# Even and odd columns in the first stage of an attention and feed-forward kernel, fewer transfers, and another order of the attention's first loads

## What is computed

```python
xn = (x - mean) / sqrt(var + 1e-5)                       # x: (4, 2048, 256)
q, k, v = xn @ Wq + bq, xn @ Wk + bk, xn @ Wv + bv       # 16 heads of 16
q, k = rope(q), rope(k)          # rot: (x0, x1) -> (-x1, x0) for each pair of columns; x*cos + rot*sin
att = softmax(q @ k.T / sqrt(256)) @ v @ Wo + bo
h = relu(s0 * concat(xn, -xn) @ sign(k0)) * 2            # to 1024
h = relu(s1 * h @ sign(k1)) * 2                          # to 1024
out = x + att + s2 * h @ sign(k2)
```

## Time and profile before

| | |
|---|---|
| median of 3 runs | 2738.48 us (2738.41 to 2739.38) |
| the profiled execution, its span | 2738.91 us, 2737.1 us |
| PE, ACT, DVE, POOL busy | 97%, 76%, 36%, 11% of the span |
| chain that ended last | PE 86% of the span |
| granted TensorE clock, mean | 0.988 |

### The profile page before, as it was taken

One profiled execution on the slowest core, in us unless ns is written; L12 is line 12 of the kernel. 1 busy time (PEld: TensorE's weight loads), 2 busy tenths in 40 slices (PEclk: granted clock), 3 DMA queues, 4 the chain that ended last, 5 costly groups with the idle time before them and its releaser, 6 DMA issues.

```text
span 2737.1 us, 49717 instructions
## 1 busy us (share of the span) xinstructions
PE 2648.9 (97%) x21063; PEld 1397.6 (51%) x21063; DVE 989.5 (36%) x1655; ACT 2083.9 (76%) x2301; POOL 299.0 (11%) x265
## 2 busy tenths in 40 slices
PE   7999499999999999999999999999999999999997
PEld 5777245454444445454545454454545454544544
DVE  7776232324242323232342334242423323242322
ACT  4556388888888887878787878888787878787883
POOL 4666100000000000000000000000000000000000
PEclk9999699999999999999999999999999999999998
DMA  8888412212222222222221222221222222222213
GB/s 256 256 259 252 114 38 55 53 52 59 59 59 59 73 54 72 55 60 72 57 71 55 72 67 75 57 77 51 73 63 55 68 60 67 63 75 59 81 26 112
DMA packets 288416, 228.67 MB, mean 84 GB/s; under 512 B 184128, under 2 KB 227904, under 8 KB 281664
## 3 DMA queue, kind: packets, MB, share of 16 engines
q1 hardware_dynamic: 279744, 217.08, 29.0%
q10 hardware_dynamic: 8448, 8.39, 0.9%
...
## 4 chain that ended last, share of the span: by engine, by line
PE 86%; issue 1%; SPq 1%; DMA 1%; DVE 0%; POOLq 0%; POOL 0%; DVEq 0%
PE ps_o L930 35%; PE ps_f L963 26%; PE ps_s L915 23%; PE ps_y L978 2%; PE ps_f L1020 0%; SPq L810 0%; DMA xT_lo<-xn_lo_d 0%; DMA probs<-rest_sum_d 0%; PE ps_y L1020 0%; DVE k_rows L1115 0%; PE ps_o L1020 0%; SPq L807 0%; DVE sums L1060 0%; DMA heads_t<-heads 0%; SPq L709 0%
## 5 line engine op out<-in xcount | busy, mean ns | idle before, releaser
L895 ACT ACTIVATE probs<-ps_s 128x1024 f32<-128x1024 f32 x2048 | 1930.0, 1033 | 472.4 <-PE ps_s L915 470.1
L930 PE MATMUL ps_o<-probs,v_ones 128*32 128x512 f32 x8192 | 1011.9, 600 | 0.0
L915 PE MATMUL ps_s<-q_rows,k_rows 50*128 50x512 f32 x4096 | 866.3, 439 | 31.8 <-DMA q_rows<-row_shift 31.0
L915 PEld LDWEIGHTS ps_s<-q_rows,k_rows 50*128 50x128 f32 x4096 | 365.0, 184 | 701.9 <-ACT probs L895 600.0
L1077 DVE COPY raw<-ps_f 128x512 f32<-128x512 f32 x256 | 165.0, 686 | 790.8 <-PE ps_f L963 790.8
L930 PEld LDWEIGHTS ps_o<-probs,v_ones 128*32 128x32 f32 x8192 | 200.7, 109 | 418.5 <-issue 296.0
L963 PE MATMUL ps_f<-h_hi,ffn_w 64*128 64x512 f32 x2048 | 406.9, 393 | 0.0
L963 PE MATMUL ps_f<-h_lo,ffn_w 64*128 64x512 f32 x2048 | 405.8, 391 | 0.0
L1039 POOL TENSOR_TENSOR heads<-heads,sums 128x512 f32<-128x512 f32 x64 | 82.4, 1288 | 2147.9 <-DVE sums L1060 2147.9
L1060 DVE RECIPROCAL sums<-sums 128x128 f32<-128x128 f32 x256 | 226.7, 924 | 1.7
L963 PEld LDWEIGHTS ps_f<-h_lo,ffn_w 64*128 64x128 f32 x2048 | 195.8, 186 | 37.3
...
## 6 DMA issues: line engine op xcount, KB each, us to landing
k_rows<-k_parts SPq DMA_DIRECT2D x128, 256.0 KB
...
q_parts<-parts SPq DMA_DIRECT2D x32, 512.0 KB, 3.7
k_parts<-parts SPq DMA_DIRECT2D x32, 512.0 KB, 5.5
k_rows<-k_parts SPq DMA_DIRECT2D x128, 128.0 KB
x_chunk<-in_x ACTq DMA_DIRECT2D x16, 512.0 KB, 6.0
xn_hi_d<-xn_hi SPq DMA_DIRECT2D x16, 512.0 KB, 4.4
xn_lo_d<-xn_lo SPq DMA_DIRECT2D x16, 512.0 KB, 5.2
```

The lines of the kernel that those rows point to most:

```text
L895: nc.scalar.activation(probs[:, s % PBUF, half * 2 * C:(half + 1) * 2 * C], ps_s[:, half].rearrange("p c n -> p (c n)"), ACT.Exp, scale=SC ...
L915: last = nc.tensor.matmul(ps_s[:, half, w], k_rows[rows, u, t * P:(t + 1) * P], q_rows[rows, u, half], start=True, stop=True)
L930: last = nc.tensor.matmul(ps_o[32 * c:32 * c + 2 * DH], v_ones[:, u, t], probs[:, s % PBUF, c * C:(c + 1) * C], start=(t == 0), stop=(t == ...
```

## The change

q and k: `project` now makes the even columns and the odd columns of all heads once each, 24 matmuls a chunk, and the rotation combines them (`products` takes each of the two blocks for both outputs; POOL subtracts for one and adds for the other). The arrays in DRAM hold 4 x 8 rows a head in place of 2 x 16, and the chunks of q are stored in another order (`COLUMNS`), so that a half of a query row is one run. The normalised x is stored once, as full fp32 (ACT copies it, `copy_x`), in one run of 4 KB a partition, and split again on DVE in `attend` (`split_x`, in round 24 of the pass before; the first by itself). v is stored in one run of 4 KB a partition and loaded with 4 transfers a head. `bn_aggr` takes the place of five small operations. v has its own PSUM banks and is made in two halves. The order of each engine in a chunk is new, with `sums` and `normalise` one chunk further ahead, and the feed-forward weights are made over chunks 4 to 11. POOL sets `k_rows` to one at the start of `prepare`. `attend` first loads rows, v and x, then the constants, and the second head only after the first rows and x have landed. `shift` is stored by 4 transfers of 128 rows in place of one of 64.

```diff
+FFN_WEIGHTS_AT = 4
+FILL = 256
+FILLS = 16 * (G * N // (P * FILL))
+COLUMNS = [CB // 2 * (r % 2) + r // 2 for r in range(CB)]
+HALF = DH // 2
+SPLIT_AT = 2 * len(BURSTS) + 4
...
@@ prepare: SP
+    def store_shift(a):
+        to = scratch["shift"][a].rearrange("g (h w n) -> w (g h) n", h=P // G, n=FILL)
+        for n in range(G * N // (P * FILL)):
+            sp.dma_start(to[n], fill[:].bitcast(F32)).then_inc(fill_stored, 16)
...
     def store_x(c):
         u = c % 2
-        sp.wait_ge(x_split, c + 1)
-        sp.dma_start(hi_out[c], x_hi[:, u].bitcast(F32)).then_inc(x_stored[u], 16)
-        sp.dma_start(lo_out[c], x_lo[:, u].bitcast(F32)).then_inc(x_stored[u], 16)
+        sp.wait_ge(x_copied, c + 1)
+        sp.dma_start(scratch["xn"][c], x_t[:, u].rearrange("p k n -> p (k n)")).then_inc(x_stored[u], 16)
...
+        to = q_out[b, j, COLUMNS[r]] if j < 2 else k_out[b, j % 2, r]
+        sp.dma_start(to, parts[:, u].bitcast(F32)).then_inc(parts_stored[u], 16)
     store_x(0)
     for c in range(NC):
         if c > 0:
+            store_parts(4 * c - 2)
             store_parts(4 * c - 1)
-        sp.wait_ge(v_ready, c + 1)
-        sp.dma_start(v_out[c // CB, c % CB], v_sb[:, c % 2].rearrange("p h t d -> p h (t d)")).then_inc(v_stored[c % 2], 16)
+        if c + 1 < NC:
+            store_x(c + 1)
         store_parts(4 * c)
         store_parts(4 * c + 1)
-        if c + 1 < NC:
-            store_x(c + 1)
-        store_parts(4 * c + 2)
+        sp.wait_ge(v_ready, 2 * c + 2)
+        sp.dma_start(scratch["v"][c], v_sb[:, c % 2].rearrange("p h t d -> p (h t d)")).then_inc(v_stored[c % 2], 16)
...
@@ prepare: ACT
+    def copy_x(c):
+        u = c % 2
+        if c >= 2:
+            act.wait_ge(x_stored[u], 16 * (c // 2))
+        nc.scalar.activation(x_t[:, u].rearrange("p k n -> p (k n)"), ps_t[:].rearrange("p k n -> p (k n)"),
+                             ACT.Copy).then_inc(x_copied, 1)
...
+        act.wait_ge(v_done, 2 * c + half + 1)
+        if c >= 2 and half == 0:
             act.wait_ge(v_stored[u], 16 * (c // 2))
-        nc.scalar.activation(v_sb[:, u].rearrange("p h t d -> p t h d"), ps_v.rearrange("p t (h d) -> p t h d", d=DH),
+        t = slice(half * TT // 2, (half + 1) * TT // 2)
+        nc.scalar.activation(v_sb[:, u, :, t].rearrange("p h t d -> p t h d"), ps_v[:].rearrange("p t (h d) -> p t h d", d=DH),
...
+    copy_x(0)
     deviation(1)
+    normalise(1)
+    deviation(2)
     act.wait_ge(weights_loaded, 16 * 6)
     for c in range(NC):
         if c > 0:
+            part(4 * c - 2)
             part(4 * c - 1)
-        values(c)
-        if c + 1 < NC:
-            normalise(c + 1)
-        part(4 * c)
-        part(4 * c + 1)
         if c + 1 < NC:
             high(c + 1)
+            copy_x(c + 1)
+        values(c, 0)
+        part(4 * c)
         if c + 2 < NC:
-            deviation(c + 2)
-        part(4 * c + 2)
-        if c == NC - CB:
-            act.wait_ge(d0_ready, 1)
-            act.wait_ge(signs_ready, 1)
-            act.wait_ge(ffn_loaded, 16 * 6)
-        if c >= NC - CB:
-            ffn_weights(c % CB)
+            normalise(c + 2)
+        part(4 * c + 1)
+        if c + 3 < NC:
+            deviation(c + 3)
+        if FFN_WEIGHTS_AT <= c < FFN_WEIGHTS_AT + FT:
+            ffn_weights(c - FFN_WEIGHTS_AT)
+        values(c, 1)
...
@@ prepare: PE
         if c > 0:
-            pe.wait_ge(v_ready, c)
+            pe.wait_ge(x_split, c)
+            pe.wait_ge(x_copied, c)
...
-        c, j = n // 4, n % 4
+        c, of = n // 2, n % 2
...
         if n >= 2:
-            pe.wait_ge(products_ready, n - 1)
-        for swapped in range(2):
+            pe.wait_ge(products_ready, 2 * n - 2)
+        for m in range(2):
             for k in range(DT):
-                at = slice((j % DT) * P, (j % DT + 1) * P)
-                w_hi, w_lo = wqk_hi[:, swapped, j // DT, k, at], wqk_lo[:, swapped, j // DT, k, at]
-                to = ps_p[:, n % 2, swapped]
+                w_hi, w_lo = wqk_hi[:, of, k, m], wqk_lo[:, of, k, m]
+                to = ps_p[:, n % 2, m]
...
     for c in range(NC):
-        project(4 * c)
-        values(c)
+        project(2 * c)
+        if c + 1 < NC:
+            turn(c + 1)
+        values(c, 0)
+        project(2 * c + 1)
+        values(c, 1)
         if c > 0:
             lengths(c - 1)
-        project(4 * c + 1)
-        project(4 * c + 2)
-        if c + 1 < NC:
-            turn(c + 1)
-        project(4 * c + 3)
...
@@ prepare: POOL
+    nc.gpsimd.memset(w["k_rows"][:].bitcast(F32), 1.0)
...
+    for m in range(2):
+        for n in range(2):
+            nc.gpsimd.tensor_tensor(wqk_lo[:, n, :, m], of_pairs[:, n, :, :, m], wqk_hi[:, n, :, m].bitcast(F32), ALU.subtract)
...
-        nc.gpsimd.tensor_tensor(turned[:, n % 3], by_cos[:, u], by_sin[:, u], ALU.add).then_inc(turn_done, 1)
+        nc.gpsimd.tensor_tensor(turned[:, n % 3], by_cos[:, u], by_sin[:, u], ALU.add if n % 2 else ALU.subtract).then_inc(turn_done, 1)
...
@@ prepare: DVE
-        nc.vector.tensor_tensor(mean2[:, u], even, odd, ALU.add)
-        nc.vector.tensor_tensor(diff[:, u], even, odd, ALU.subtract)
-        nc.vector.tensor_tensor(var[:, u], stats[:, u, :, 2], stats[:, u, :, 5], ALU.add).then_inc(stat_step, 1)
-        dve.wait_ge(stat_step, 2 * c + 1)
-        nc.vector.scalar_tensor_tensor(out=diff[:, u], in0=diff[:, u], scalar=D / 4.0, in1=diff[:, u],
-                                       op0=ALU.mult, op1=ALU.mult).then_inc(stat_step, 1)
-        dve.wait_ge(stat_step, 2 * c + 2)
-        nc.vector.tensor_tensor(var[:, u], var[:, u], diff[:, u], ALU.add).then_inc(var_ready, 1)
+        for t in range(TT):
+            last = nc.vector.bn_aggr(moments[:, u, t], stats[:, u, t])
+        last.then_inc(var_ready, 1)
...
-        c, j, u = n // 4, n % 4, n % 2
-        dve.wait_ge(proj_ready, n + 1)
+        c, pair, out, u = n // 4, n // 2, n % 2, n % 2
+        if out == 0:
+            dve.wait_ge(proj_ready, pair + 1)
         if n >= 2:
             dve.wait_ge(turn_done, n - 1)
-        nc.vector.scalar_tensor_tensor(out=by_cos[:, u], in0=ps_p[:, u, 0], scalar=bqk[:, 0, j:j + 1], in1=cos[:, here(c)],
+        of = pair % 2
+        nc.vector.scalar_tensor_tensor(out=by_cos[:, u], in0=ps_p[:, of, out], scalar=bqk[:, of, out:out + 1], in1=cos[:, here(c)],
                                        op0=ALU.add, op1=ALU.mult)
-        nc.vector.scalar_tensor_tensor(out=by_sin[:, u], in0=ps_p[:, u, 1], scalar=bqk[:, 1, j:j + 1], in1=sin[:, here(c)],
+        nc.vector.scalar_tensor_tensor(out=by_sin[:, u], in0=ps_p[:, of, 1 - out], scalar=bqk[:, of, 1 - out:2 - out], in1=sin[:, here(c)],
                                        op0=ALU.add, op1=ALU.mult).then_inc(products_ready, 1)
...
-        dve.wait_ge(x_high, c + 1)
+        dve.wait_ge(x_copied, c + 1)
...
     for c in range(NC):
         products(4 * c)
+        products(4 * c + 1)
+        if c + 1 < NC:
+            low(c + 1)
+        if c + 3 < NC:
+            sums(c + 3)
+        products(4 * c + 2)
+        if c + 3 < NC:
+            factors(c + 3)
+        products(4 * c + 3)
         if c > 0:
             keep_norms(c - 1)
-        products(4 * c + 1)
-        if c + 2 < NC:
-            sums(c + 2)
-        products(4 * c + 2)
-        if c + 1 < NC:
-            low(c + 1)
-        products(4 * c + 3)
-        if c + 2 < NC:
-            factors(c + 2)
...
@@ load_rows and attend
-    return (scratch[name].rearrange("a (g d) n -> g a d n", d=DH) for name in ("k", "q"))
+    return (scratch[name].rearrange("am (g e) n -> g am e n", e=HALF) for name in ("k", "q"))
...
-    shift = scratch["shift"].rearrange("a g (h w n) -> g w a h n", w=2, n=C)
-    q_half = scratch["q"].rearrange("a (g d) (h w n) -> g a w d h n", d=DH, w=2, n=C)
+    shift = scratch["shift"].rearrange("a g (w n) -> g w a n", w=2)
+    q_flat = q_rows.rearrange("p h n -> p (h n)")
     for w in range(2):
 at = GROUP_ROWS * w
+here = slice(w * N // 2, (w + 1) * N // 2)
 sp.dma_start(k_rows[at:at + 2 * DH, :].bitcast(F32), k_head[g]).then_inc(loaded, 16)
-sp.dma_start(k_rows[at + 2 * DH:at + AUG, :].bitcast(F32), k_head[g, 0]).then_inc(loaded, 16)
-sp.dma_start(q_rows[at:at + DH].bitcast(F32), q_half[g, 0, w]).then_inc(loaded, 16)
-sp.dma_start(q_rows[at + DH:at + 2 * DH].bitcast(F32), q_half[g, 0, w]).then_inc(loaded, 16)
-sp.dma_start(q_rows[at + 2 * DH:at + AUG].bitcast(F32), q_half[g, 1, w]).then_inc(loaded, 16)
-sp.dma_start(q_rows[at + AUG:at + ROWS].bitcast(F32), shift[g, w]).then_inc(loaded, 16)
+sp.dma_start(k_rows[at + 2 * DH:at + AUG, :].bitcast(F32), k_head[g, 0:2]).then_inc(loaded, 16)
+sp.dma_start(q_flat[at:at + DH].bitcast(F32), q_head[g, 0:2, :, here]).then_inc(loaded, 16)
+sp.dma_start(q_flat[at + DH:at + 2 * DH].bitcast(F32), q_head[g, 0:2, :, here]).then_inc(loaded, 16)
+sp.dma_start(q_flat[at + 2 * DH:at + AUG].bitcast(F32), q_head[g, 2:4, :, here]).then_inc(loaded, 16)
```

(39 more changed lines are left out.)

143 lines of the change are left out of this document (67 added, 76 removed).

## The result

The changed kernel takes **2670.81 us** (median of 4 runs, 2669.19 to 2672.23); the kernel before takes 2738.93 us (4 runs, 2738.41 to 2740.60) beside it. The ratio is 0.975, 95% interval 0.9733 to 0.9767: 2.5% faster. The profiled execution of the changed kernel took 2669.19 us, its span is 2667.4 us, against a span of 2737.1 us before: 69.7 us less.

The account below looks back on a forecast made before the run. PE was taken to bound both stages, with a chain through ACT, DVE and POOL deciding `prepare` after the change. Terms -71.7 - 3.3 + 0.3 - 1.5 + 7.5 = -68.7 us against 2738.9 gave 2670 us, range 2648 to 2712 us.

Parts of the forecast that it names:

- The chain of a chunk (11.7 us): `prepare`: the chain through ACT, DVE and POOL, closed by POOL's addition, sets a chunk's period, 11.7 us against 16.38.
- The signs' block: `prepare`: the block of the signs takes 4.6 us of DVE once, now in a full chain: 3 us.
- The transfers shrink from 4.0 to 3.5 MB a chunk, all in long runs but the load of x; at the 403 GB/s of a slice full of 2 KB runs that is 9.1 us: `prepare`: a chunk's transfers need 9.1 us, near the other resources' 10 us, so the chain decides.
- rival 3: `prepare`: a longer chain, as by held `bn_aggr` or late stores, at 14 us: +28 us, 2698 us; chance 10%.
- The term of `prepare`: To the end of the last `turned`: -75.0 us predicted, with 15 periods giving -71.7 and the start -3.3.
- The start and the end of `prepare`: Half the lower parts of the weights at the start: -3.3 us; the block's end, shorter `fill`, three more SP issues: +0.3 us.
- The start of `attend`: Memset's 3.47 us go, but outer counts limit engines, rows take 19.0 us instead of 12.7: -1.5 us, between -7 and +5.
- Each pass of `attend` (+7.5 us): `attend`: late x holds DVE's split and PE stalls 0.5 us a pass, 15 passes: +7.5 us, between 0 and 47.
- the delay of x: `attend`: x, issued behind SP's held store and slower rows, comes 3.7 us later, between 2.3 and 6.3.
- my slack of 3.15 us: `attend`: x may come 3.15 us later for nothing before DVE's copy delays PE's next group.
- Rival 1: `attend`: x so late that `prepare`'s gain is lost, from 5.1 us of stall a pass; 2768 us at 7 us; 4%.
- Rival 5: `prepare`: PE, now with gaps, is granted 1.2 GHz: +121 us, 2791 us, slower; chance 1%.

Follow-up runs that it names:

- runs 1: Changed kernel, but of v and the turned x only chunk 0 is stored, and `attend` reads that chunk everywhere: 2658.53 us (ratio 0.9707).
- run 7: Changed kernel with key rows' setting back in `attend`, three buffers for loaded x, eight for parts, `d0` in the split weights' tile: 2666.06 us (0.9731).
- run 3: Changed kernel with DVE's `low` starting after `high`, and ACT's plain copy of x moved behind the first half of v: 2683.08 us (0.9796).
- run 4: Changed kernel with the setting of the key rows to one put back on DVE at the start of `attend`: 2673.92 us (0.976).
- run 9: Changed kernel with every transfer of key and query rows cut into pieces of 8 rows: 2661.19 us (0.9721).
- run 10: Changed kernel with each pass's x issued only after PE's ten steps of the third head, about 5.8 us later: 2768.24 us (1.0106).

## Why the prediction was right in the sum, and where its steps failed

**The chain of a chunk (11.7 us)** was right, in its path and to 0.3 us: 11.39 us from chunk 8 on where no transfer interferes (runs 1 and 7). These rows of run 7 show the stretch between the third and the fourth product in two periods, which begin with `high` at 142.56 and at 153.95:

```profile
148.84 1.30 POOL L503 TENSOR_TENSOR turned<-by_cos,by_sin 128x512 f32<-128x512 f32 x1 [1.06 <-DVE by_sin L550]
149.78 0.18 DVE L535 RECIPROCAL rstd<-std 128x4 f32<-128x4 f32 x1 [1.02 <-ACT std L319]
149.99 0.16 DVE L537 SCALAR_TENSOR_TENSOR shift_ln<-moments,rstd 128x4 f32<-128x4 f32 x1
...
160.22 1.30 POOL L503 TENSOR_TENSOR turned<-by_cos,by_sin 128x512 f32<-128x512 f32 x1 [1.06 <-DVE by_sin L550]
160.60 0.18 DVE L535 RECIPROCAL rstd<-std 128x4 f32<-128x4 f32 x1 [0.46 <-ACT std L319]
160.82 0.72 DVE L537 SCALAR_TENSOR_TENSOR shift_ln<-moments,rstd 128x4 f32<-128x4 f32 x1
```

In both, POOL's addition follows the third product, and `shift_ln` ends with it, at 150.15 and 161.54, as the prediction had it; the fourth product, POOL and the fourth part close the period. POOL waits for DVE as foreseen, 1.06 us ahead of the third sum and 0.18 us ahead of the fourth. What the prediction lacked is the branch through ACT that run 3 laid open. It arrives at nearly the same time: in the first period DVE waits 1.02 us for the square root and `shift_ln` then needs only its own 0.16 us, in the second the root is there 0.6 us earlier, and the period is the same. That this branch costs no more than 0.1 us here is luck. In the sum itself, 7.75 + 0.17 + 1.30 is 9.2 and not the 9.0 of the text; `bn_aggr` x4 takes 0.38 us with POOL at work beside it, where I had 0.45.

Smaller terms of the stage were off. The signs' block makes two periods of 13.95 and 13.18 us in run 7, 4.3 us more than two of 11.4, where I had 3 us. Of the three periods of 10.2 us at the end only the last came (10.17); the two before it are 11.39 and 11.38 us. And in two of the eight chunks that make feed-forward weights ACT works 2.7 us on them (79.50 to 82.16 in run 7), where I had 1.4 us and let them fit into its wait: these periods are 12.23 and 12.30 us.

**"The transfers shrink from 4.0 to 3.5 MB a chunk, all in long runs but the load of x; at the 403 GB/s of a slice full of 2 KB runs that is 9.1 us"** is the step that failed in `prepare`. The bytes did not turn out to be the bound, but the slice is the best of many, and I took from it that transfers in a shorter period would be as quick as before. The landings went from 3.8 to 7.0 us and from 6.1 to 9.4 us. With two buffers for x and four for the parts that is too late in five of the eleven periods: 12.30 us on average from chunk 4 to 15 in place of the 11.44 of run 7 ((186.89 - 61.02) / 11, chunk 4 at 61.02), 11 x 0.86 = 9.5 us. It is the "stores that come back late" of my rival 3, and the load of x beside them, with a smaller price than its 28 us, and I gave it 10% beside a forecast that should have contained it. The term of `prepare` was 9.6 us too good for that.

**The start and the end of `prepare`** were about right: the first projection comes at 14.98 us in place of 18.42, 3.4 us earlier (predicted 3.3). From the last `turned` to SP's load I had 3.2 us less, measured are 4.8; run 4 shows 4.3 of it as the key rows' setting.

**The start of `attend`** stood on the outer count. The rows took 20.7 us from SP's first load to the first scores, where I had 1.5 + 19.0 us, and the feed-forward network began 28.1 us behind that load, where I had 28.3. Run 9 shows the outer count at work: with 8 rows outside, the share of 232 to 236 us goes from 0.20 to 0.50 and 7.6 us come back. The rule of the Trainium skill (DMA: Bandwidth & Descriptors, section "Why a DMA increments its semaphore by 16 and not by 1") gives 8 of 16 engines for it, and the trace agrees. One detail was off: DVE's split waited for `bo`, the last transfer of all (it landed at 254.1), not for x (252.4).

**Each pass of `attend` (+7.5 us)** was wrong: the passes are 1.3 us shorter in all. The mechanism is there, as run 10 shows, but it never starts. In the seventh pass, shifted by 70.25 us (PE's next group, 1307.84 in the earlier trace rows, is at 1237.59):

```profile
1225.82 3.94 SPq L833 DMA_DIRECT2D heads_t<-heads  x4
1229.87 0.35 SPq L827 DMA_DIRECT2D xT_lo<-xn_d  x1
```

```profile
1233.47 0.69 DVE L1084 CAST xT_hi<-xT_lo 128x1024 fp32r<-128x1024 f32 x1 [15.79 <-DMA xT_lo<-xn_d]
...
1235.34 1.28 DVE L1103 COPY raw<-ps_f 128x512 f32<-128x512 f32 x2
```

x is issued 1229.87 + 70.25 - 1297.38 = 2.7 us later than before, not 3.7; it lands in 3.6 us, not 4.1; and PE goes on when the first bank is copied, as run 10 shows, 0.6 us earlier than I counted. So DVE idles 15.79 us and its copy starts 1.6 us before it would cost anything. The step that failed is the delay of x, 3.7 us against 2.7 measured: this alone is less than my slack of 3.15 us and leaves no stall. The slack was too small as well; it is 3.8 us.

**The rivals.** Rival 1 is real but was priced too low. I had it decide from 5.1 us of stall a pass; with the clock's share it is 5.1 x 4.0 / 6.5 = 3.1 us. Rival 5 did not come: PE stayed near full clock in `prepare`, 0.99 between 35 and 195 us, though some of its gaps were longer than the 2 us that I named (3.70 us before 49.31, 3.29 us before 83.21). The forecast held because 10 us of late transfers were set off by 9 us of stalls that did not happen. That is luck, and the range, not the point, was what the argument had earned.
